# Attention on one core: the score products for a unit's row maxima, dealt to the unit's steps by their number of queries in place of evenly

## What is computed

```python
q_lat = jnp.einsum('bqhd,hdl->bhql', q, k_eff)
attn = jnp.einsum('bhql,bkl->bhqk', q_lat, c_kv) / sqrt(hs)   # 16 heads of 16
causal = jnp.tril(jnp.ones((T, T), dtype=bool))
attn = jnp.where(causal[None, None], attn, -jnp.inf)
attn = jax.nn.softmax(attn, axis=-1)
y_lat = jnp.einsum('bhqk,bkl->bhql', attn, c_kv)
```

## Time and profile before

| | |
|---|---|
| time, median of 3 runs | 1286.22 us (1285.48 to 1290.86) |
| the profiled execution's own time | 1286.14 us |
| its span, first to last instruction | 1284.0 us |
| mean granted TensorE clock | 0.969 |
| attention, first to last `values` matmul | 88.95 to 608.05 us |
| one of the units 8 to 13 | 30.5 to 31.1 us |
| one of the units 0 to 7 (with projections) | 32.2 to 37.3 us |

### The profile page before, as it was taken

One profiled execution on the slowest core, in us unless ns is written; L12 is line 12 of the kernel. 1 busy time (PEld: TensorE's weight loads), 2 busy tenths in 40 slices (PEclk: granted clock), 3 DMA queues, 4 the chain that ended last, 5 costly groups with the idle time before them and its releaser, 6 DMA issues.

```text
span 1284.0 us, 32364 instructions
## 1 busy us (share of the span) xinstructions
PE 1166.2 (91%) x13250; PEld 717.1 (56%) x13250; DVE 857.1 (67%) x2072; ACT 662.6 (52%) x1449; POOL 391.0 (30%) x614
## 2 busy tenths in 40 slices
PE   6889999999999999998799997768899778899995
PEld 3334444444434444433688885436676666688884
DVE  6686868777788888871563367797867563465255
ACT  4446666676666666666432237745554222342232
POOL 5421414141300000002333125645564223643210
PEclk9899999999999999999899998989999999999998
DMA  6754425454564444400000000102111110000003
GB/s 205 165 138 51 88 30 95 59 90 61 90 121 51 51 51 51 51 3 2 1 1 1 1 26 15 31 9 57 38 37 32 40 30 12 3 1 1 1 9 123
DMA packets 78755, 61.65 MB, mean 48 GB/s; under 512 B 41360, under 2 KB 65552, under 8 KB 78480
## 3 DMA queue, kind: packets, MB, share of 16 engines
q1 hardware_dynamic: 77456, 57.18, 24.8%
q10 hardware_dynamic: 1152, 2.41, 0.6%
HBM read 38.20 MB, written 20.97 MB: 46 GB/s over the span
## 4 chain that ended last, share of the span: by engine, by line
PE 32%; DVE 10%; issue 5%; POOL 3%; ACT 1%; DMA 0%; POOLq 0%; DVEq 0%; SPq 0%
PE psum L1044 8%; PE psum L1050 7%; PE psum L1059 2%; PE psum L1588 2%; PE psum L1528 2%; DVE d_products L1725 2%; DVE d_inverse L1730 2%; PE psum L1566 2%; DVE d_conv_sum L1800 1%; PE psum L1557 1%; PE psum L1523 1%; PE psum L1510 1%; PE psum L1514 1%; PE psum L257 1%; PE psum L1537 1%
## 5 line engine op out<-in xcount | busy, mean ns | idle before, releaser
L751 ACT ACTIVATE weights<-psum 128x512 f32<-128x512 f32 (+1 forms) x608 | 318.3, 584 | 156.9 <-PE psum L652 154.8
L652 PE MATMUL psum<-q_stack,k_stack 99*128 99x512 bf16 (+3 forms) x768 | 224.0, 328 | 1.8 <-ACT weights L751 1.0
L574 PE MATMUL psum<-k_stack,q_stack 96*128 96x512 bf16 (+3 forms) x768 | 209.2, 328 | 5.3 <-DVE maxima L809 2.0
L809 DVE TENSOR_REDUCE maxima<-psum 128x1 f32<-128x512 f32 (+2 forms) x304 | 189.2, 683 | 12.5 <-PE psum L574 11.9
L806 DVE CUSTOM_DVE_ANT_0 unread<-psum,mask_scores 128x384 bf16<-128x384 f32 (+1 forms) x256 | 159.5, 623 | 50.3 <-PE psum L574 26.8
L669 PE MATMUL psum<-weights,v_rows 128*17 128x512 f32 (+3 forms) x1536 | 162.0, 494 | 0.1
L545 POOL TENSOR_TENSOR residual<-residual,att_o 128x256 f32<-128x256 f32 x32 | 23.3, 727 | 350.0 <-DVE att_o L842 350.0
L1044 PE MATMUL psum<-f_xT,f_weights_hi 128*128 128x512 f32 x384 | 122.9, 402 | 4.2 <-DVE f_hidden L1160 2.1
L652 PEld LDWEIGHTS psum<-q_stack,k_stack 99*128 99x128 bf16 x768 | 72.6, 98 | 90.1 <-ACT weights L751 41.3
L1086 ACT ACTIVATE f_gates<-psum,ffn_biases 128x512 f32<-128x512 f32 x72 | 49.5, 689 | 140.4 <-PE psum L1050 132.6
L1128 DVE TENSOR_TENSOR f_state<-f_gates 128x512 f32<-128x512 f32 x32 | 27.2, 849 | 116.5 <-POOL f_gates L1003 73.8
(11 more groups left out here) (168 smaller groups left out, 2238.8 us busy)
## 6 DMA issues: line engine op xcount, KB each, us to landing
qk_parts<-a_parts SPq DMA_DIRECT2D x32, 384.0 KB, 3.6
q_stack<-qk_parts SPq DMA_DIRECT2D x90, 128.0 KB, 6.6
k_stack<-qk_parts SPq DMA_DIRECT2D x90, 128.0 KB, 7.3
residual<-in_x SPq DMA_DIRECT2D x8, 512.0 KB, 7.4
out_x<-residual SPq DMA_DIRECT2D x8, 512.0 KB, 3.0
ffn_weights<-in_ffn_w ACTq DMA_DIRECT2D x1, 2048.0 KB, 11.7
systems<-d_attnT_k_kb_v SPq DMA_DIRECT2D x32, 64.0 KB, 1.8
d_systems<-systems SPq DMA_DIRECT2D x4, 512.0 KB, 3.5
```

The lines of the kernel that those rows point to most:

```text
L574: m = e.matmul(out[:, i * width:(i + 1) * width], self.qst[st][0:self.ROWS, h, qb * P:(qb + 1) * P], self.kst[st][0:self.ROWS, h, k0:k0 + ...
L652: m = e.matmul(out[:, j * width:(j + 1) * width], self.kst[st][0:self.ROWS + self.MAX_ROWS, h, kb * P:(kb + 1) * P], self.qst[st][0:self.R ...
L751: e.activation(self.weights[n % 2][:, heads[0]:heads[-1] + 1, 0:width], bank[self.score_bank[n, i]][:, 0:len(heads) * width].rearrange("p ...
L809: e.tensor_reduce(to, scores.rearrange("p (h x) -> p h x", h=len(heads)), AXIS_X, ALU.max, negate=True).then_inc(*s["max_red"].did(u, w_at))
```

## The change

Before, each of a unit's 12 steps got a twelfth of the 38 products, 3 or 4. Now a step gets them in proportion to its number of queries, rounded up on the running sum. By steps 0 to 11 that is 4, 3, 3, 3, 3, 3, 4, 3, 3, 3, 3, 3 before and 5, 3, 2, 1, 4, 4, 5, 4, 4, 3, 2, 1 now. Nothing else is changed: the products, their sequence, the banks of the ring and the distance of two products between w = 37 and the `negmax` item are the same.

```diff
--- before.py
+++ after.py
@@ -371,8 +371,10 @@
             if g > 4:
                 for j in range(2):
                     self.during[first - 8 + 2 * j].append(("norm", g, slice(2 * j, 2 * j + 2)))
+        passed = 0
         for n, (u, kb, qc) in enumerate(self.steps):
-            self.during[n] += take(lead + -(-per * (n + 1) // len(self.unit_steps)))
+            passed += self.span(n)[1]
+            self.during[n] += take(lead + -(-per * passed // sum(self.span(i)[1] for i in range(len(self.unit_steps)))))
             if kb == (qc + 1) * TPG - 1:
                 self.during[n + 3].append(("out", u, qc))
         self.during[len(self.steps) - 10].append(("first",))
```

## The result

The changed kernel took 1292.93 us (median of 12 runs, 1289.07 to 1295.56), the kernel before 1286.42 in the same measurement (12 runs, 1281.48 to 1291.86). The ratio is 1.0048, 95% interval 1.0035 to 1.0062, or 6.2 us (4.5 to 8.0). So it is slower, by an amount that lies at the bound of 0.5%; the time forecast, 1290.0, is 3 us low. One run of experiment 7, 1490.82 us at a lower granted clock, is left out of that experiment's numbers.

The account below looks back on a forecast made before the run. PE was taken to bound the attention, so only its waits count: losses of 7.7, 1.8 and 1.3 us less gains of 2.2, 2.5 and 2.2 made +3.9 on 1286.14, hence 1290.0 us, range 1284 to 1298.

Parts of the forecast that it names:

- The transpose, eight units: `negmax` transpose in units 5 and 7 to 13: PE waits 0.87 us for DVE, taken as 0.96, 7.7 us lost.
- the walk: PE's and DVE's work added up from step 6's `out` transposes to the `negmax` transpose: 8.29 against 9.16 us.
- Units 0 to 4 and 6: `negmax` transpose in units with a projection in steps 6 and 8: wait of 0.3 us each, 1.8 us lost.
- rival 2: DVE is further behind than walked, partly through layer norm statistics in projection units: +11 us, 1297; chance 0.27.
- Unit 14: `negmax` transpose with no further products to cover it: some 1.3 us lost on top of today's wait.
- Step 5: Fourth score bank's wait for ACT shrinks from 0.24 to 0.1 us or less: 2.2 us gained over 15 units.
- Step 1: Products' waits for a ring bank that DVE has not read: 2.5 of 3.6 us counted as gained.
- The DMAs: First score of a unit no longer waits for the DMAs of the maxima: 2.2 us gained.
- The gain (3): DVE has room at the transpose and waits go: chance 0.10 around 1283.5 us, 0.06 below 1279.8.
- The clock (4): New waits halve PE's clock in each unit, +26, about 1315 us: chance 0.02; 0.02 for a later stage's fall changing.

Follow-up runs that it names:

- experiment 7: Changed kernel with two alternating `unread` buffers and the combine as a reduce over the pair of maxima: 1276.31 us, ratio 0.9936 to the kernel before.
- experiment 1: Changed kernel with the `negmax` transpose one product later: 1284.41 us, ratio 1.0001 to the kernel before.
- experiment 4: Changed kernel with two products of step 8 moved to step 9, so the transpose falls into step 9: 1283.13 us, ratio 0.9993 to the kernel before.
- experiment 3: Changed kernel with two alternating `unread` buffers for the custom instruction's output: 1280.74 us, ratio 0.9962 to the kernel before.
- experiment 2: Kernel before with the `negmax` transpose right behind w = 37, not two products later: 1297.62 us, ratio 1.0105 to the kernel before.
- Experiment 6: Changed kernel with the combine as a reduce over the pair of maxima, not a two-input minimum: 1289.47 us in one run.
- Experiment 8: Changed kernel with the `negmax` transpose six products behind w = 37, not two: 1359.29 us in one run.
- second trace: Changed kernel measured once more, unaltered, against the kernel before: 1290.89 us, ratio 1.0044.

## Why the prediction was right, step by step

**The transpose, eight units.** The step was a wait of 0.87 us, with 0.09 more for safety; it measured 0.74 to 0.75. Both sides of the walk came out 0.06 to 0.07 off: DVE needed 9.10 us from the `out` transposes to the L584 matmul (476.78 to 485.88), where the walk had 9.16, and PE would have needed 9.10 - 0.74 = 8.36, where it had 8.29. The 0.09 was not lost twice. 8 x 0.75 = 6.0 for 7.7. Experiments 1 and 4 take the wait away by place and experiment 3 by DVE's speed, and experiment 2 shows that a wait here is lost in full: the cause is shown.

**Units 0 to 4 and 6.** 0.3 each, 1.8 in all, was forecast; 0.23 in units 0, 2 and 3, but 0.56 in unit 1 and 0.80 and 0.79 in units 4 and 6: 2.84. Here the step was mis-sized: the walk took the combine at 0.18 us, and in units 4 and 6 it lasts 0.75 behind GpSimd. Experiment 6 shows this, as the wait falls to 0.24. The kernel before had part of it already, 0.31 and 0.30 us at the transpose of these units, which the prediction did not see; what is new in the six units is 2.2 us. In unit 1 the layer norm's statistics stand in the same queue, two instructions of 0.75 and 0.30 us between the custom ones:

```profile
146.38 0.75 DVE L223 BATCH_NORM_STATS2 ln_stats<-residual 128x6 f32<-128x256 f32 x2
147.04 0.30 DVE L227 BATCH_NORM_AGGREGATE ln_moments<-ln_stats 128x2 f32<-128x6 f32 x2
```

That is rival 2's mechanism, and it costs 0.33 us in one unit, not 0.5 in half of them; that it is the statistics alone wasn't tried.

**Unit 14.** 1.3 on top of today's wait: it went from 0.76 to 1.79, +1.0.

**Step 5.** A gain of 15 x 0.15 = 2.2 was forecast. By spacing the wait was 0.17 us in six units and 0.22 or 0.23 in nine, together 3.1; after, unit 8 alone has one, 0.1. So 3.0 us: a product's slot took away the whole wait, not two thirds of it.

**Step 1.** 2.5 us counted as gained. By spacing, before had 0.34 us in unit 2, 0.25 in each of 8, 10, 12 and 13, and 0.61 in 11, together 1.95; after, unit 11 alone has 0.33. So 1.6 us; the 3.6 of the weight load's row overstated what PE lost, as the 12.8 above does. To this comes the ring in units 1 and 3, step 6, where 0.26 us each are new. By the prediction's own words a wait for the ring of over 0.2 us in step 6 speaks against it; it stands in these two units and in none of the others.

**The DMAs.** 2.2 us were to go. By spacing 0.97, 0.80 and 0.6 in three units went and 0.1 or less in each of six others, 2.9 us.

**The sum.** At the transposes 10.6 - 1.4 = +9.2 (forecast 10.8), 0.5 for the ring in step 6, 0.8 ahead of the first `values` (not forecast), less 3.0, 1.6 and 2.9: +3.0, against 4.0 from end to end. Spacings that are off by less than 0.05 us, and 0.3 us behind the transpose of unit 14, are not in it. The sum of +3.9 was good in part by luck: the eight units and unit 14 were 2.0 us dearer in the forecast and step 1 gained 0.9 more there, while the other six units, the ring in step 6 and the start were 1.7 cheaper, and step 5 and the DMAs gained 1.5 less.

**The rest of the 6.2 us.** The first trace has 1.7 of its 6.0 us from a clock that the changed kernel doesn't set. In the median of many runs such chance should vanish, and 4.0 lies just outside of the first interval (4.5 to 8.0) and inside the second (3.3 to 8.1). A leftover of 1 to 2 us stays open. The stages behind the attention start 4 us later and have other stretches at half clock (half of the time at 0.50 is 30.6 us before, 32.5 and 32.2 in the two traces of after), but three traces don't show that this is more than chance. Experiments 1 and 4 have a leftover too: their attention is 2.7 and 4.2 us shorter than before as traced, and their times are no lower (ratios 1.0001 and 0.9993, whose intervals reach down to 0.9985 and 0.9973, 1.9 and 3.5 us). No run separates a cost of the new distribution outside the attention from the clock.

**The rivals.** The larger loss (2) needed an average wait of 0.9 us at the transpose; it is 10.6 / 15 = 0.71. The gain (3) needed DVE idle before w = 36; it wasn't. What it describes is the changed kernel of experiment 3. The clock (4) didn't fall: the granted clock is 1.00 in the unit shown, though it has a wait of 0.74, and the wait of 1.79 in unit 14 brought none in this kernel: the next fall stands 5.1 us behind the start of the last unit, as it did before. The Trainium skill ("TensorE: Matmul & The Clock Gate", Part 1) says that an idle array goes back to half rate. The gaps that it warns of are longer than 0.9 us, so the prediction read more into it than it says. Experiment 8 agrees with it behind waits of 2.2 us; behind waits of 0.74 us no fall came, in any of the eight units of two traces.

## What to carry to other kernels

A product that is dealt to another step takes along everything whose place is counted in products: here a transpose moved up by 1.9 us of PE's work, and that cost more than the better balance brought. Moving the dependent item on its own, one product later, takes the loss away (ratio 1.0001). Speeding up the engine that feeds it makes the same distribution a gain of 0.4%, with both DVE edits 0.6%. To price such a move, start both engines at the last moment at which the feeding one was idle and walk them to the meeting point; where a third engine may share a port with the feeding one, take its instruction's length from the units in which that engine runs too.

## What the runs showed of the hardware

**A VectorE instruction with two SBUF inputs is held by GpSimd.** The view of groups, the 15 combines of the attention, first as TENSOR_TENSOR in the changed kernel, then as TENSOR_REDUCE in experiment 6 (busy us, mean ns of one):

```profile
L816 DVE TENSOR_TENSOR negmax<-maxima 128x16 f32<-128x16 f32 x15 | 3.8, 252 | 0.5
```

```profile
L816 DVE TENSOR_REDUCE negmax<-maxima 128x16 f32<-128x32 f32 x15 | 2.8, 187 | 0.5
```

As TENSOR_TENSOR it took 174 to 177 ns where no GpSimd TENSOR_TENSOR of 128x512 ran, and up to 1156 ns (in experiment 3) where one did, ending about 0.03 us behind it; as a reduce 186 to 189 ns in every unit. The Trainium skill ("GPSIMD Engine Reference", Specifications) names such a contention, for VectorE instructions with two inputs from SBUF; the traces agree, and add that the short instruction pays the rest of the long one.

**One buffer that nobody reads cost 0.23 us an instruction.** The custom instruction started every 0.84 us with one buffer and every 0.61 with two, 0.71 and 0.48 for 384 columns. Its busy time, 0.69 us, tells neither.

**The clock.** It did not fall behind single waits of 0.7 us (changed kernel) and of 1.0 to 1.5 us (experiment 2). Behind waits of 2.2 us it fell in nine of eleven places (experiment 8), up to 1.6 us after PE's work began again. The wait of 1.8 us in unit 14 goes either way: no fall followed it within 10 us in the changed kernel, its second trace and experiments 4 and 6; in experiment 1 the clock fell 0.8 us behind it, and in experiment 8 0.2 us behind. Here is the place in experiment 1, the transpose and the window of the fall:

```profile
572.32 0.27 PE L584 MATMUL psum<-identity,negmax 128*32 128x128 f32 x1 [1.63 <-DVE negmax L816]
```

```profile
573.10:576.50 3.40, 3.40 (x20) 1.02 (x16) 0.61 (x3) 1.85 (x5) 0.00 (x0) 0.50 0.04 7
```

So a wait of this length is a risk and not a certainty, and what decides it no run here shows.
